# Recurrent attention: the output's share of the state is read from PSUM by ScalarE instead of VectorE

## What is computed

```python
def attend(h):
    q = h @ Wq.T
    scores = jnp.einsum('bc,bsc->bs', q, context)
    alpha = jax.nn.softmax(scores, axis=-1)
    ctx = jnp.einsum('bs,bsc->bc', alpha, context)
    return jnp.tanh(jnp.concatenate([ctx, h], axis=-1) @ Wout.T + b_out)

def step(carry, x_t):
    h, c, attn = carry
    inp = jnp.concatenate([x_t, attn], axis=-1)
    gates = inp @ W_ih.T + b_ih + h @ W_hh.T + b_hh
    i, f, g, o = jnp.split(gates, 4, axis=-1)
    c = jax.nn.sigmoid(f) * c + jax.nn.sigmoid(i) * jnp.tanh(g)
    h = jax.nn.sigmoid(o) * jnp.tanh(c)
    attn_out = attend(h)
    return ((h, c, attn_out), attn_out)
```

## Time and profile before

| what | us |
|---|---|
| median of 3 runs | 694.99 |
| the three runs | 694.54, 694.99, 697.08 |
| the profiled execution, its own time | 696.79 |
| the profiled execution, first to last instruction | 695.0 |

### The profile page before, as it was taken

How to read it: one execution, slowest core, us unless ns; L and a number is a source line. 1 busy time by engine, 2 the same in 40 slices (tenths; PEclk the granted TensorE clock), 3 DMA queues, 4 the chain that set the end, 5 groups by cost and what they waited for, 6 DMA issues and landing times.

```text
span 695.0 us, 21604 instructions
## 1 busy us (share of the span) xinstructions
PE 569.2 (82%) x8469; PEld 440.0 (63%) x8469; DVE 480.8 (69%) x1894; ACT 298.3 (43%) x851; POOL 163.3 (23%) x209
## 2 busy tenths in 40 slices
PE   3958768577996689999998999996688988898857
PEld 2625544255884588888888888885366656665535
DVE  1567828965444677777777777773589898989882
ACT  2857825135555433323323233332454555554501
POOL 3234543108000000000000000000653466336600
PEclk9969989798998555555555555555899999999995
DMA  8800000001002000000000000000000000000000
GB/s 339 367 1 1 1 4 1 2 11 33 1 1 91 3 3 0 0 0 0 0 0 0 0 0 0 0 0 1 0 1 1 0 2 1 0 1 1 0 1 8
DMA packets 6056, 15.26 MB, mean 22 GB/s; under 512 B 2640, under 2 KB 3288, under 8 KB 5504
## 3 DMA queue, kind: packets, MB, share of 16 engines
q1 hardware_dynamic: 5296, 11.19, 4.4%
q10 hardware_dynamic: 720, 3.55, 1.3%
HBM read 14.60 MB, written 0.13 MB: 21 GB/s over the span
## 4 chain that ended last, share of the span: by engine, by line
PE 37%; DVE 33%; ACT 14%; issue 11%; POOL 2%; DMA 1%; DVEq 1%; SPq 0%; ACTq 0%; POOLq 0%
PE bank L1688 7%; PE bank L1597 6%; PE bank L1756 5%; ACT esp L678 3%; PE bank L1548 2%; DVE ssum L1144 2%; ACT a L664 2%; ACT e L680 2%; PE bank L1535 2%; DVE rz L1181 2%; DVE zs L1179 2%; DVE asp L1134 2%; DVE opre L1120 2%; DVE w L1201 2%; DVE esp L1163 1%
## 5 line engine op out<-in xcount | busy, mean ns | idle before, releaser
L474 POOL MEMSET ctxT<- 128x128 f32 x1 | 0.3, 316 | 303.9 <-DVE xres L1188 303.9
L1597 PE MATMUL bank<-esp,qblk 128*128 128x1 f16 (+1 forms) x2048 | 66.6, 166 | 0.7 <-ACT esp L678 0.7
L1597 PE MATMUL bank<-hsp,kT 128*128 128x2 f16 x2048 | 63.6, 166 | 2.2 <-DVE hsp L1172 1.7
L664 ACT ACTIVATE a<-opre 128x4 f32<-128x4 f32 x64 | 13.1, 205 | 115.3 <-DVE opre L1132 115.3
L1597 PEld LDWEIGHTS bank<-esp,qblk 128*128 128x128 f16 x2048 | 61.3, 104 | 1.2 <-ACT esp L678 1.1
L1597 PEld LDWEIGHTS bank<-hsp,kT 128*128 128x128 f16 x2048 | 60.0, 104 | 3.1 <-DVE hsp L1169 1.7
L1214 DVE SCALAR_TENSOR_TENSOR T<-bank,bct,T 128x256 f32<-128x256 f32 x112 | 46.4, 473 | 2.2 <-PE bank L1769 2.2
L1597 PE MATMUL bank<-asp,lsp 128*128 128x4 f16 x768 | 30.7, 168 | 16.3 <-DVE asp L1134 16.3
L1597 PEld LDWEIGHTS bank<-asp,lsp 128*128 128x128 f16 x768 | 25.4, 105 | 27.8 <-DVE asp L1134 27.7
L1201 DVE TENSOR_TENSOR_SCAN qblk<-ctxT,bank 128x512 f32<-128x512 f32 x32 | 37.7, 1207 | 5.7 <-PE bank L1756 5.3
L1201 DVE TENSOR_TENSOR_SCAN w<-kT,bank 128x512 f32<-128x512 f32 x32 | 37.5, 1205 | 1.1 <-PE bank L1756 1.1
(11 more groups left out here) (327 smaller groups left out, 1399.2 us busy)
## 6 DMA issues: line engine op xcount, KB each, us to landing
w<-in_w_dram SPq DMA_DIRECT2D x2, 2048.0 KB
ctxT<-in_ctxT_dram SPq DMA_DIRECT2D x8, 256.0 KB, 13.5
wqkv<-in_qkvT_dram ACTq DMA_DIRECT2D x1, 1536.0 KB, 12.0
w<-in_mw_dram SPq DMA_DIRECT2D x1, 1024.0 KB, 5.2
lw<-in_lw_dram SPq DMA_DIRECT2D x1, 960.0 KB, 19.7
rows<-in_rows_dram ACTq DMA_DIRECT2D x1, 772.0 KB, 8.2
wqkv<-in_fw_dram SPq DMA_DIRECT2D x1, 532.0 KB, 3.5
T<-in_mask_dram ACTq DMA_DIRECT2D x1, 512.0 KB, 6.2
```

The source lines that it names most:

```text
L664: act.activation(a32[:, g, :], opre[:, g, :], ACT.Tanh).then_inc(sem["at_32"], 1)
L1597: return pe.matmul(out, lhsT, rhs, start=start, stop=stop, skip_group_check=True)
```

## The change

`oh` is now written by ScalarE: an activation with the function Identity, with the same scale and bias, that stands last in ScalarE's `half`, behind `tanhc`. It signals a new semaphore, `oh_sb`. VectorE's instruction is gone, and its addition to `opre` now waits for `oh_sb` as well. TensorE waits for `oh_sb` of the half before ahead of the first of the three products that overwrite bank 5. VectorE has 16 instead of 18 counted steps in a turn. At the start of the program the semaphore `eps_ready` is dropped, and the two memsets that signalled it count as VectorE's steps.

```diff
-        LSTM_STEPS = 18
+        LSTM_STEPS = 16
@@ scalar engine
-            act.wait_ge(sem["eps_ready"], 2)
             act.wait_ge(sem["d_par"], 48)
@@ scalar engine, half(), last
                     act.activation(tanhc[:, g, :], c2[:, g, :], ACT.Tanh, scale=0.5).then_inc(sem["c_tanh"], 1)
+                if main:
+
+                    g, t = main
+                    act.wait_ge(sem["oh_ps"], nth(g, t))
+                    act.activation(oh[:, g, :], bank[5][:, 0:BH], ACT.Identity, bias=v("bout"), scale=loh[:, :]) \
+                       .then_inc(sem["oh_sb"], 1)
@@ vector engine
-            dve.memset(eps5[:, :], 1e-5).then_inc(sem["eps_ready"], 1)
-            dve.memset(eps6[:, :], 1e-6).then_inc(sem["eps_ready"], 1)
+            step.mark(dve.memset(eps5[:, :], 1e-5))
+            step.mark(dve.memset(eps6[:, :], 1e-6))
@@ vector engine, half()
                     step.sync()
+                    dve.wait_ge(sem["oh_sb"], nth(g, t))
                     dve.tensor_tensor(opre[:, g, :], opre[:, g, :], oh[:, g, :], ALU.add).then_inc(sem["o_pre"], 1)
@@
-                    dve.wait_ge(sem["oh_ps"], nth(g, t))
-                    step.mark(dve.tensor_scalar(oh[:, g, :], bank[5][:, 0:BH], loh[:, :], v("bout"), ALU.mult, ALU.add))
                     dve.wait_ge(sem["z_ps"], nth(g, t))
@@ tensor engine, half()
                 h_gates(g)
+                if g:
+                    pe.wait_ge(sem["oh_sb"], nth(0, t))
+                elif not (isinstance(t, int) and t == 0):
+                    pe.wait_ge(sem["oh_sb"], nth(1, t - 1))
                 for k, n in MEETS:
                     ins = mm(bank[5][:, 0:BH], weight(k, 8), hsp[:, g, n, :], start=(k == 1), stop=(n == 1))
```

More of the change, by code:

```diff
@@ L281, in build @@
              "xw_ps", "xw_sb", "k_proj", "k_sq", "k_var", "k_rstd", "k_hat", "k_done", "v_proj", "v_evac",
-             "eps_ready", "mask_ready", "qblk_ready", "x_score", "x_max", "x_exp", "x_rz", "x_norm", "x_tr", "x_pt", "x_ptd", "x_pv",
+             "mask_ready", "qblk_ready", "x_score", "x_max", "x_exp", "x_rz", "x_norm", "x_tr", "x_pt", "x_ptd", "x_pv",
              "x_oT", "x_o", "xb_ready", "x_res")
@@ L291, in build @@
              "l_gxlow", "l_zero", "g_ps", "g_act", "c_new", "c_tanh", "h_hi", "h_lo", "s_hi", "m_c", "m_t", "m_d",
-             "s_ps", "s_sum", "e_hi", "e_32", "e_lo", "oh_ps", "z_ps", "v_ps", "o_pre", "at_hi", "at_32", "at_lo",
+             "s_ps", "s_sum", "e_hi", "e_32", "e_lo", "oh_ps", "oh_sb", "z_ps", "v_ps", "o_pre", "at_hi", "at_32", "at_lo",
              "y_st", "y_tr")
```

## The result

| kernel | median, us | runs | ratio to before, 95% interval |
|---|---|---|---|
| before | 695.5 | 9 | |
| changed | 691.98 | 9 | 0.9948, 0.9935 to 0.9962 |

The change wins 3.5 us, between 2.6 and 4.5. The forecast was 687.7, a gain of 7.3; the time is inside its range and the direction is right, but the gain is half of what was forecast.

What follows compares the result with a forecast made beforehand. A chain of dependences through VectorE's instructions, no full engine, was taken as the bound. 45 halves x 0.09 = 4.1 plus 16 pass ends x 0.20 = 3.2 gave -7.3 us, 694.99 to 687.7; range 685.5 to 692.8.

Steps and rivals of the forecast that it cites:

- Part (1): VectorE loses `oh`: 0.20 us freed ahead of `zs`; inside a pass `mc` gains only 0.06, then waits 0.14 for scores.
- Part (2): VectorE's addition of `oh` to `opre` follows `mc` after 0.09 us, not 0.12; 0.09 gained per half inside a pass.
- Rival A: VectorE's addition follows `mc` only after 0.20 us, because of the sequencer's arithmetic; total -2.3, 692.7 us; chance 0.12.
- Part (3): Everything behind the addition keeps its distances; a half goes from 3.65 to 3.56 us, bound by TensorE's path to the scores.
- Rival B: The scores are no bound, as TensorE's path has hidden slack; all 61 halves gain 0.20 us: 682.8; chance 0.05.
- Part (4): At a pass's end VectorE's still-stand of 0.54 us moves with `rz`; the whole 0.20 is gained, in 16 places.
- Part (5): ScalarE's 64 added activations, 0.20 to 0.31 us each, fit its 1.69 us idle before the next tanh and cost nothing.
- Part (6): TensorE's wait for `oh_sb`, met some 3 us earlier, costs 0; upper bound 0.17 plus 0.10 us.
- rival C: TensorE's wait on the thirteenth product breaks its stream, costing 0.22 us in each half: 697.7 us; chance 0.08.
- Rival D: Identity is missing from ScalarE's loaded table, which each half reloads twice: over +75 us, 770; chance 0.01.
- Part (7): The semaphore dropped at the program's start lies outside any wait that the chain shows: 0.

## Why the prediction was half right

**Part (1), the slot of `oh` and the scores behind it:** right. 0.20 came free, and inside a pass 0.12 of it went into a wait for the scores, for a forecast 0.14 (`mc` 0.20 behind the product instead of 0.08; 0.60 behind the scores for a forecast 0.61). The price of 0.13 for the slot, from the Trainium skill's page VectorE: DVE Perf Modes, the TRN2 errata, doesn't fit: the whole 0.20 shows at a pass's end in the run without `oh`, 4.17 to 3.97. That 0.13 is also the lower bound of the slot in the forecast's 687 to 691, although the prediction says that no estimate uses it; no run shows it.

**Part (2), the addition, is the step that failed.** It took the distance to `mc` as 0.09 from two instructions with one condition each. With one condition that is right, 0.10 in two runs. What it left out is that the change gives the addition a second condition, and that this is an instruction of its own for the sequencer: 0.07 to 0.08 in each half. The order of instructions listed the two conditions on one row, and I read them as one. With the prediction's own rows, 0.17 in place of 0.09 inside a pass and 0.18 in place of 0.12 at its start, the sum is 45 x 0.01 + 16 x 0.14 = 2.7; with the halves as measured it is 45 x 0.02 + 16 x 0.12 = 2.8. That is what the trace has: from the first tanh `a` to the last the stage takes 234.3 us for 237.2 (the kernel before stands first). The other 0.6 of the measured 3.5 lie within the interval.

```profile
L664 ACT ACTIVATE a<-opre x64: 205/205/206, 236.7 to 473.9; 128x4 f32<-128x4 f32 x64
```

```profile
L663 ACT ACTIVATE a<-opre x64: 205/206/206, 236.0 to 470.3; 128x4 f32<-128x4 f32 x64
```

The Trainium skill has the rule, Perfetto Trace Analysis, the section Identifying Dependency Chains: an instruction that waits on several engines may get semaphore instructions put in front of it. The trace agrees, with 0.02 for the instruction and 0.07 for its effect. The section gives no price; with the price of these runs the term is 45 x 0.07 + 16 x 0.08 = 4.4, and 7.3 less 4.4 is 2.9.

**Rival A** came within 0.7 us (692.7) by luck. It blamed the sequencer's arithmetic behind a waiting `mc`. That arithmetic does start only behind `mc` there, but in the run without `oh` it did so too and the distance was 0.10, not 0.20. A made the halves inside a pass 0.04 too slow, and left the pass's end untouched, where the new wait costs 0.08; the two errors nearly cancel (-2.3 for the stage's -2.9).

**Part (3), nothing else moves:** right, tanh to `asp` to scores kept their distances (addition to the next scores 2.86 before and after). But "now bound by TensorE's path to the scores" was true only while the addition stood behind `mc`; with the addition first the half went to 3.46. **Rival B** is wrong for the changed kernel, and its 0.20 a half is about what the reordered one gets (3.65 to 3.46, 4.17 to 3.96).

**Part (4), the still-stand moves with `rz`:** right, 0.54 before and after, 16 times, 8.1 us. **Part (5), ScalarE's cover:** right, though `oh` takes 0.34, above both bounds I had named; ScalarE's idle time ahead of the next tanh went from 1.69 to 1.42, and nothing waits for it. **Part (6), TensorE's wait at nothing:** right, so rival C falls (its own sum, 0.17 + 0.10 less a slot of 0.04, is 0.23 and not 0.22, which changes nothing). **Rival D** falls with the profile: no table load in the loop. **Part (7)**, the dropped semaphore at the start, was not tried by itself; the first addition starts between 234.1 and 238.1 us in the nine profiles, so a small gain ahead of the stage can't be seen in them.

## What to carry to other kernels

Count the semaphore conditions of each instruction on the chain that sets the time: here the second one was an instruction of its own. It cost its full price where the sequencer came to it late, with arithmetic for another wait to do as well, and nothing where the instruction waited for a result anyway. So put a met wait in front of an instruction that hangs on a result still under way, and test where it stands after every other change, since the place that hides it moves. And when an instruction is taken from a chain, look at what now stops the ones behind it: here the order of two independent instructions, worth nothing before, was worth 8 us afterwards. Some 3 us of these are the order itself, and the rest came because the new order also hid the wait.

## What the runs showed of the hardware

- A second condition on a VectorE instruction inside the loop, met long before, costs 0.07 to 0.08 where the sequencer reaches it late (`mc` to addition 0.10 with one condition, 0.17 with two). It costs nothing behind a result that is awaited for 0.20 anyway (3.46 a half with the wait there, 3.49 with it at `zs`). On TensorE one condition on a product in a running row costs nothing (0.54 for fifteen either way).
- In the written-out halves, where the waits compare with constants and need no arithmetic, the second condition is free: the addition follows `mc`, which waits there too, after 0.09 with two conditions (changed kernel, first) and after 0.09 with one (the run without `oh`, second):

```profile
235.74 0.17 DVE L1131 TENSOR_REDUCE mc<-bank 128x4 bf16<-128x16 f32 x1
235.83 0.15 DVE L1138 TENSOR_TENSOR opre<-opre,oh 128x4 f32<-128x4 f32 x1
```

```profile
235.92 0.17 DVE L1126 TENSOR_REDUCE mc<-bank 128x4 bf16<-128x16 f32 x1
236.01 0.15 DVE L1132 TENSOR_TENSOR opre<-opre,oh 128x4 f32<-128x4 f32 x1
```

  With the 0.10 for arithmetic alone and the 0.17 for both, all four cases are there: either one hides behind `mc`, and only the two in a row don't. The halves differ in more than the arithmetic, and it was not taken out by itself.
- An activation with Identity and both scale and bias per partition, 4 columns from PSUM, takes 0.34, more than the 0.27 of the tanh of 16 columns with a scale alone:

```profile
L689 ACT ACTIVATE oh<-bank,vec,loh x64: 336/337/338, 234.4 to 468.6; 128x4 f32<-128x4 f32 x64
```

```profile
L671 ACT ACTIVATE gact<-bank,lgate 128x16 f32<-128x16 f32 x64 | 17.5, 274 | 45.6 <-PE bank L1601 45.6
```
